# Cached keys turned once per page and stored, values copied by page ahead: paged attention with a LoRA layer behind it, on one core

## The chip, the cores and the metric

One core of a Trainium2 chip runs the kernel. The metric is the device time of one execution in microseconds.

## The reference, cut to what matters

Two layers on x (8 batches of 128 tokens, 512 wide), all in float32. The first is attention over a paged cache: 32 query heads, 8 key/value heads of 128, so one key/value head serves four query heads (REP). A batch has 16 cache pages of 32 keys, named by a block table, and 128 new keys.

```python
q = _rope(_rmsnorm(x @ Wq.T)); k = _rope(_rmsnorm(x @ Wk.T)); v = x @ Wv.T
kc = k_cache[block_table].reshape(bsz, 512, 8, 128)      # 16 pages of 32 keys
vc = v_cache[block_table].reshape(bsz, 512, 8, 128)
k_all = concatenate([kc, k], axis=1); v_all = concatenate([vc, v], axis=1)
scores = where(valid, einsum('bqhd,bkhd->bhqk', q, k_all) * SCALE, -1e30)
o = einsum('bhqk,bkhd->bqhd', softmax(scores), v_all)
x = x + o.reshape(bsz, 128, 4096) @ Wo.T
```

The second layer is a 512 x 512 product with a gated mixture of two of eight low-rank experts. It runs after the last attention step and is not touched.

## The kernel before, in words

The program is written out by hand: each engine has its own list of instructions, and semaphores order them. The work is a loop of G = 64 steps s, one for each pair of key/value head s // 8 and batch s % 8. One step has 640 keys (512 cached, 128 new) and 4 query heads. Products are made in three passes of float32r: every operand is split by ACT into a high part (a Copy that rounds) and by DVE into a low part (`low`, L857: full minus high), and PE multiplies high by high, high by low and low by high (L320).

PE's order in step s (`step`, L1423): scores of heads 0 and 1; the query projection of group s + 2; scores of head 2; the product O of step s - 1 with the values; scores of head 3; the turns (transposes) of the probabilities of heads 0, 1, 2 (T0, T1, T2; `turn_probs`, L1390); the output projection Y; the turns of the queries, cached keys and new keys of group s + 1 (`turn_queries` L1356, `turn_cached_keys` L1368, `turn_new_keys` L1339); the key/value projection of s + 2; the turns of head 3's probabilities (T3) and of the new keys' ones (TN).

PSUM has four banks for this beside the scores' four, and each has several users in a fixed cycle (`BANKS`, L72); `wait_bank` (L296) makes PE wait until the user before has been copied out, by the table `FREES` (L288). QT is free when DVE has made qt_lo, Q when ACT has copied the queries (a_q).

```python
BANKS = (("Q", "T0", "QT", "T3"), ("O", "Y", "TN"), ("T1", "KTC"), ("T2", "KV"))
```

ACT's order in step s (L731): new keys and values copied, squares, exp and norm of heads 0 and 1, queries of s + 2 (`queries`, L642), exp and norm of head 2, the copy of O (L761), values (L698), probs 0 to 2 (L687), exp and norm of head 3, the split of w, then the high parts of turned queries, cached keys, new keys (L664 to L674), and the probabilities of T3 and TN. DVE (L1007) follows with the low parts, the row maxima (L952), the reciprocals (L962) and the rope's sine product (L927). POOL (L520) makes the rope's cosine product, the norms' weights and v_lo.

Cached keys and values come as one array `kv` in DRAM, rows of 256 numbers (128 of the key, 128 of the value), by head, page and slot. `kv_raw` in SBUF holds two groups. Groups 0 to 11 (GATHERED) are gathered by POOL with indirect DMAs, four for a group (L492), two steps ahead. Groups from 12 on are loaded by SP (`cached_pages`, L415): 16 DMAs for a group, one for each page, 32 rows of 1 KB, the page number read from SBUF into a register. SP's iteration s (L449) also loads a piece of w and of wo, and the split x of group s + 4 (`fetch_x`, L385), each behind waits that say its buffer is free; SP's queue keeps this order.

## Time and profile before

| | us |
|---|---|
| median of 3 runs | 1154.88 (1154.5 to 1155.11) |
| the profiled execution | 1157.93 |
| its span | 1156.1 |
| PE busy | 1144.5 (99%) |
| ACT busy | 927.9 (80%) |
| DVE busy | 907.1 (78%) |
| POOL busy | 550.3 (48%) |

The page of the profile gives the busy time of each engine, in all and in 40 slices, then the DMA queues, the chain of work that ended last, and the costliest groups of instructions. PE is matmul, PEld the weight load of PE, which overlaps it; "line" is a line of the kernel. In a timeline a row begins with start and length in us; rows of one kind are merged (x12), and brackets give the idle time before a row and who ended it. On ACT and DVE the next instruction may start some 0.1 us before the one before it has ended, so the distance of two starts is what an instruction costs its engine.

### The profile page before, as it was taken

What the parts mean: (1) busy time and instruction counts of PE and PEld (TensorE: products, weight loads), DVE (VectorE), ACT (ScalarE), POOL (GpSimd) and SP (SyncE); (2) the same over time, 40 slices, a digit from 0 to 9 for tenths busy, and PEclk for the clock granted to TensorE, in tenths of its full rate; (3) what the DMA queues carried; (4) which work ended last, traced back from release to release, by engine and by line L of the source; (5) the groups of instructions that cost most, each with busy time, mean ns of one, the idle gap of its engine ahead of it and who ended that gap; (6) DMA issues with size and microseconds to landing.
All of it is one profiled execution on the core that took longest, in us unless ns stands there. A gap on an engine that the chain in (4) does not pass through costs nothing.

```text
span 1156.1 us, 23349 instructions
## 1 busy us (share of the span) xinstructions
PE 1144.5 (99%) x6960; PEld 1030.6 (89%) x6960; DVE 907.1 (78%) x1883; ACT 927.9 (80%) x1833; POOL 550.3 (48%) x573
## 2 busy tenths in 40 slices
PE   8999999999999999999999999999999999999998
PEld 7888988989999998998998999899899899899997
DVE  8977788777778778777777877877877777777756
ACT  6887888888888888888888888888888888887751
POOL 5766766454444445345445444444534544544400
PEclk9999999999999999999999999999999999999999
DMA  7514322122223223222222322222222222221001
GB/s 244 166 61 138 102 88 96 58 88 80 77 87 93 65 87 90 68 87 88 86 72 87 94 63 87 92 66 88 89 69 86 87 84 71 85 81 53 23 1 73
DMA packets 86733, 98.31 MB, mean 85 GB/s; under 512 B 18768, under 2 KB 65744, under 8 KB 86480
## 3 DMA queue, kind: packets, MB, share of 16 engines
q1 hardware_dynamic: 84016, 90.40, 25.6%
q0 software_dynamic: 2304, 6.29, 1.7%
q8 instruction: 57, 0.93, 0.3%
q14 instruction: 68, 0.56, 0.2%
q10 hardware_dynamic: 288, 0.13, 0.0%
HBM read 90.45 MB, written 6.29 MB: 84 GB/s over the span
## 4 chain that ended last, share of the span: by engine, by line
PE 91%; ACT 3%; DVE 2%; issue 2%; DMA 0%; SPq 0%; POOL 0%; ACTq 0%; DVEq 0%; POOLq 0%
PE ps_s L1386 19%; PE ps_w L327 18%; PE ps_w L328 18%; PE ps_w L329 18%; PE ps_w L1397 9%; PE ps_w L1365 2%; PE ps_w L1406 2%; PE ps_w L1372 2%; ACT ps L679 1%; PE ps_s L1306 1%; DVE m L934 1%; PE ps_s L1340 1%; ACT ps L685 0%; DMA m<-wqkv 0%; DVE o_lo L858 0%
## 5 line engine op out<-in xcount | busy, mean ns | idle before, releaser
L685 ACT ACTIVATE ps<-ps,recip 128x640 f32<-128x640 f32 x256 | 213.3, 834 | 61.9 <-DVE recip L965 61.6
L858 DVE TENSOR_TENSOR pt_lo<-ps_w,pt_hi 128x512 fp32r<-128x512 f32 x322 | 204.4, 684 | 56.3 <-ACT pt_hi L690 53.4
L679 ACT ACTIVATE ps<-ps,negmax 128x640 f32<-128x640 f32 x256 | 213.3, 833 | 25.1 <-DVE negmax L958 24.0
L958 DVE CUSTOM_DVE_ANT_0 ps<-ps_s,mask 128x640 f32<-128x640 f32 x256 | 209.7, 820 | 8.0 <-issue 2.7
L507 POOL TENSOR_SCALAR meansq<-sumsq 128x5 f32<-128x5 f32 x63 | 12.8, 203 | 394.8 <-DVE sumsq L925 392.7
L690 ACT ACTIVATE pt_hi<-ps_w 128x512 fp32r<-128x512 f32 x256 | 139.5, 600 | 73.1 <-PE ps_w L1397 70.2
L327 PE MATMUL ps_w<-w_hi,xt_hi 128*128 128x512 f32 (+1 forms) x496 | 172.1, 347 | 0.0
L328 PE MATMUL ps_w<-w_lo,xt_hi 128*128 128x512 f32 (+1 forms) x496 | 167.3, 337 | 0.0
L329 PE MATMUL ps_w<-w_hi,xt_lo 128*128 128x512 f32 (+1 forms) x496 | 167.3, 337 | 0.0
L1397 PE MATMUL ps_w<-cst,ps 128*128 128x128 f32 x1024 | 133.2, 273 | 0.3 <-DVE qt_lo L858 0.2
L515 POOL TENSOR_TENSOR rot<-u,cos 128x640 f32<-128x640 f32 x63 | 100.6, 1597 | 66.2 <-DVE u L980 66.2
L533 POOL TENSOR_TENSOR rot<-rot,m 128x320 f32<-128x320 f32 x126 | 107.8, 879 | 50.6 <-DVE m L934 50.4
L327 PE MATMUL ps_w<-pt_hi,v_hi 128*128 128x512 f32 x320 | 125.4, 392 | 0.0
L328 PE MATMUL ps_w<-pt_lo,v_hi 128*128 128x512 f32 x320 | 125.2, 391 | 0.0
L329 PE MATMUL ps_w<-pt_hi,v_lo 128*128 128x512 f32 x320 | 124.5, 389 | 0.0
L1386 PE MATMUL ps_s<-kt_hi,qt_hi 128*128 128x320 f32 x512 | 122.2, 320 | 1.6 <-DVE kt_lo L858 1.6
L1397 PEld LDWEIGHTS ps_w<-cst,ps 128*128 128x128 f32 x1024 | 117.1, 141 | 1.7 <-ACT ps L685 0.9
L1386 PE MATMUL ps_s<-kt_hi,qt_lo 128*128 128x320 f32 x512 | 117.2, 310 | 0.0
L1386 PE MATMUL ps_s<-kt_lo,qt_hi 128*128 128x320 f32 x512 | 116.9, 309 | 0.0
L327 PE MATMUL ps_w<-wo_hi,o_hi 128*128 128x512 f32 x256 | 105.3, 411 | 2.6 <-DVE o_lo L858 2.4
L934 DVE TENSOR_TENSOR m<-u,sin 128x640 f32<-128x640 f32 x64 | 103.9, 1623 | 0.0
L329 PEld LDWEIGHTS ps_w<-w_hi,xt_lo 128*128 128x128 f32 x496 | 93.3, 188 | 10.0
(186 smaller groups left out, 2640.4 us busy)
## 6 DMA issues: line engine op xcount, KB each, us to landing
kv_raw<-kv SPq DMA_DIRECT2D x832, 32.0 KB, 1.6
xt_hi<-xsplit SPq DMA_DIRECT2D x56, 256.0 KB
xt_lo<-xsplit SPq DMA_DIRECT2D x56, 256.0 KB
w_raw<-wqkv SPq DMA_DIRECT2D x56, 192.0 KB, 3.4
wo_raw<-wo SPq DMA_DIRECT2D x56, 128.0 KB, 3.3
y<-xT SPq DMA_DIRECT2D x8, 256.0 KB, 3.1
y<-x SPq DMA_DIRECT2D x8, 256.0 KB
out<-y SPq DMA_DIRECT2D x8, 256.0 KB, 2.2
```

What stands on the lines that cost most here:

```text
L327: nc.tensor.matmul(out_ap, a_hi, b_hi, start=start and k == 0, stop=False)
L328: nc.tensor.matmul(out_ap, a_hi, b_lo, start=False, stop=False)
L329: last = nc.tensor.matmul(out_ap, a_lo, b_hi, start=False, stop=stop and k == n - 1)
L533: nc.gpsimd.tensor_tensor(rot[:, :, a:a + HALF], rot[:, :, a:a + HALF], m2[:, :, c:c + HALF], ALU.add).then_inc(p_rot, 1)
L679: nc.scalar.activation(ps[:, h, :], ps[:, h, :], ACT.Exp, bias=negmax[:, s % 2, h:h + 1], scale=-1.0, accum_out=rowsum[:, s % 2, h:h + 1]) ...
L685: nc.scalar.activation(ps[:, h, :], ps[:, h, :], ACT.Copy, scale=recip[:, s % 2, h:h + 1]).then_inc(a_norm, 1)
L690: nc.scalar.activation(pt_hi[:, 0:CT, h, :], probs_bank(s, h).rearrange("p (t q) -> p t q", t=CT), ACT.Copy).then_inc(a_pt, 1)
L858: return nc.vector.tensor_tensor(out_ap, full, hi.bitcast(F32), ALU.subtract)
L934: nc.vector.tensor_tensor(m2[:], u[:], sin[:, g % B, :].unsqueeze(1).to_broadcast([P, NH, D]), ALU.mult).then_inc(d_m2, 1)
L958: nc.vector.tensor_tensor_reduce(out=halves(ps[:, h, :]), in0=ps_s[:, h % 2, :, 0:KH], in1=halves(mask[:, s % B, :]), scale=-SCALE, scalar ...
L1386: last = nc.tensor.matmul(ps_s[:, h % 2, half, 0:KH], a, c[:, half * KH:(half + 1) * KH], start=n == 0, stop=n == 2)
L1397: last = nc.tensor.transpose(probs_bank(s, h)[:, t * S:(t + 1) * S], ps[:, h, t * P:(t + 1) * P], ident)
```

## The change

From the third head on (TURNED = 2, groups KG = 16 and up) cached keys are no longer turned in the step that uses them. The cache holds 64 pages a head. In steps 5 to 52 PE turns, once for each head, eight natural pages (256 rows: two transposes, `turn_natural_keys`), ACT copies them to `k_turned`, and SP stores them by page in a DRAM array `kT` (128 x 32 numbers a page). From group 16 on SP loads a group's 16 turned pages from `kT` into the keys' half of `kv_raw` (`key_pages`; 128 rows of 128 B each), and ACT and DVE split them right from SBUF; PE's four transposes of the cached keys are not there in those steps. The values of heads 2 to 7 are copied in DRAM in steps 5 to 12, page by page in the order of the block table (`copy_values`: for each batch 16 DMAs, each 6 heads x 32 rows x 512 B), into `paged`; a group's values are then one load (`load_values`, 4 x 128 rows of 512 B). POOL gathers groups 0 to 15 in place of 0 to 11.

Order changes: the probabilities of heads 0 to 2 are turned and split in the order 1, 0, 2 (TURNS); ACT's copy of the queries stands behind the copy of O, not before exp of head 2; from group 16 on the cached keys' split stands on ACT and DVE between probs and exp of head 3 (DVE: reciprocal), and ACT's split of w behind the new keys and the natural copy. PE's natural turn stands behind the new keys' turn, in the bank of the scores of heads 1 and 3; the scores of head 1 of the next step wait for ACT's copy of it. The negated sines are not made; sine and its negative become one table, with a subtract for the first half of the rope.

```diff
-GATHERED = 12
+TURNED = 2
+KG = TURNED * B
+TPAGES = PAGES // B
+TT = TPAGES * PSIZE // P
+AHEAD = 3
+TURNS = (1, 0, 2)
+COPY = 5
...
+        k_nat = sb("k_nat", [P, TT, D])
+        k_turned = sb("k_turned", [P, TPAGES, PSIZE])
+        kT = nc.dram_tensor("kT", (HK * PAGES, D, PSIZE), F32).ap()
+        paged = nc.dram_tensor("paged_values", (B, HK - TURNED, NPP, PSIZE, D), F32).ap()
...
-        sin = sb("sin", [P, B, D])
+        sin = sb("sin", [P, B, HALF])
...
+        def naturals(s):
+
+            n = s + AHEAD
+            return n if KG - B <= n < (HK - 1) * B else None
+
+        def key_cols(g):
+            return kv_raw[:, g % 2, :, 0:D]
+
+        def tiles_of(keys):
+            return keys.rearrange("p (t q) -> p t q", t=CT)
+
+        def naturals_bank():
+            return ps_s[:, 1, 0, 0:TT * P]
...
+        def turn_number(s, h):
+
+            return TURNS.index(h) + 1 if s > 0 and h in TURNS else h + 1
...
-            def cached_pages(g):
-
-                wait(sp, pe_ktc, g - 2)
+            def natural_keys(s):
+                n = naturals(s)
+                if n is None:
+                    return
+                if n > KG - B:
+                    sp.wait_ge(pe_nat, n - (KG - B))
+                row = (n + B) * TPAGES * PSIZE
+                sp.dma_start(k_nat[:], kv[row:row + TT * P, 0:D].rearrange("(t p) d -> p t d", t=TT)).then_inc(s_knat, 16)
+
+            def keep_keys(s):
+                n = naturals(s)
+                if n is None:
+                    return
+                sp.wait_ge(a_nat, n - (KG - B) + 1)
+                page = (n + B) * TPAGES
+                sp.dma_start(kT[page:page + TPAGES].rearrange("n d s -> d n s"), k_turned[:]).then_inc(s_kstored[(n // B + 1) % 2], 16)
+
+            def page_numbers(b, part):
+                at = I_BLOCK + b * CT
+                _, ids = nc.values_load_multi_w_load_instructions(
+                    cin[part * PSIZE:part * PSIZE + 1, at:at + CT], engines=[mybir.EngineType.SP], min_val=0, max_val=PAGES - 1,
+                    skip_runtime_bounds_check_because="pages of the table are numbered from 0 to PAGES - 1")
+                return ids
+
+            def copy_values(b):
+
+                pages = kv.rearrange("(h n s) d -> n h s d", h=HK, s=PSIZE)
+                for part in range(PPT):
+                    ids = page_numbers(b, part)
+                    for t in range(CT):
+                        sp.dma_start(paged[b, :, t * PPT + part, :, :],
+                                     pages[bass.ds(ids[t], 1), TURNED:HK, :, D:2 * D].rearrange("o h s d -> (o h) s d")
+                                     ).then_inc(s_paged, 16)
+
+            def load_values(g):
+                if g == KG:
+                    sp.wait_ge(s_paged, 16 * B * NPP)
                 wait(sp, p_v, g - 2, 2)
-                pages = kv.rearrange("(n s) d -> n s d", s=PSIZE)
+                sp.dma_start(kv_raw[:, g % 2, :, D:2 * D],
+                             paged[g % B, g // B - TURNED].rearrange("n s d -> (n s) d").rearrange("(t p) d -> p t d", p=P)
+                             ).then_inc(s_values[g % 2], 16)
+
+            def key_pages(g):
+
+                wait_stored(sp, g // B, B)
+                wait(sp, d_ktc, g - 2)
                 for part in range(PPT):
-                    at = slice(part * PSIZE, (part + 1) * PSIZE)
-                    b = I_BLOCK + g % B * CT
-                    _, ids = nc.values_load_multi_w_load_instructions(
-                        cin[part * PSIZE:part * PSIZE + 1, b:b + CT], engines=[mybir.EngineType.SP], min_val=0, max_val=PAGES - 1,
-                        skip_runtime_bounds_check_because="pages of the table are numbered from 0 to PAGES - 1")
+                    ids = page_numbers(g % B, part)
                     for t in range(CT):
-                        sp.dma_start(kv_raw[at, g % 2, t, :], pages[bass.ds(ids[t] + g // B * PAGES, 1)].rearrange("o s d -> (o s) d")
-                                     ).then_inc(s_pages[g % 2], 16)
+                        sp.dma_start(kv_raw[:, g % 2, t, part * PSIZE:(part + 1) * PSIZE],
+                                     kT[bass.ds(ids[t] + g // B * PAGES, 1)].rearrange("o d s -> (o d) s")
+                                     ).then_inc(s_keys[g % 2], 16)
...
+                if s > 0:
+                    keep_keys(s - 1)
+                natural_keys(s)
...
-                if GATHERED <= s + 2 < G:
-                    cached_pages(s + 2)
+                if 0 <= s - COPY < B:
+                    copy_values(s - COPY)
+                if KG <= s + 2 < G:
+                    key_pages(s + 2)
+                    load_values(s + 2)
```

ACT's step afterwards (the other engines alike):

```diff
-                if has(g2):
-                    queries(g2)
                 if has(s) and s >= G - HB + 1:
                     final_turn(s - (G - HB + 1))
                 if has(s):
@@ -759,24 +851,33 @@
                     wait(act, pe_o, s - 1)
                     wait(act, pe_y, s - 2)
                     nc.scalar.activation(o_hi[:], bank("O"), ACT.Copy).then_inc(a_o, 1)
+                if has(g2):
+                    queries(g2)
                 if has(s):
 
                     values(s)
-                    probs(s, 0)
-                    probs(s, 1)
-                    probs(s, 2)
+                    for h in TURNS:
+                        probs(s, h)
                     if s in W_MID:
                         w_split(W_MID[s])
                     if s in WO_MID:
                         wo_split(WO_MID[s])
+                    if KG <= g1 < G:
+                        cached_keys(g1)
                     exps(s, 3)
                     norm(s, 3)
-                for n in W_AT.get(s, ()):
-                    w_split(n)
+                if g1 < KG:
+                    for n in W_AT.get(s, ()):
+                        w_split(n)
                 if has(g1):
                     turned_queries(g1)
-                    cached_keys(g1)
+                    if g1 < KG:
+                        cached_keys(g1)
                     new_keys(g1)
+                natural_keys(s)
+                if g1 >= KG:
+                    for n in W_AT.get(s, ()):
+                        w_split(n)
```

## Rows read from the trace of the kernel before

**Rows 1.** The page's part 1: busy us, share of the span, instructions, by engine
```profile
PE 1144.5 (99%) x6960; PEld 1030.6 (89%) x6960; DVE 907.1 (78%) x1883; ACT 927.9 (80%) x1833; POOL 550.3 (48%) x573
```

**Rows 2.** The stage table: us, busy us (instructions) by engine, clock, DMA share, GB/s
```profile
600.00:1000.00 400.00, 400.00 (x2446) 361.26 (x2445) 316.33 (x634) 332.69 (x658) 181.27 (x186) 1.00 0.27 81
```

**Rows 3.** Timeline of PE in step 34: start us, us, line, output and inputs
```profile
603.22 0.54 PE L1386 MATMUL ps_s<-kt_hi,qt_hi 128*128 128x320 f32 x2
...
611.88 0.39 PE L329 MATMUL ps_w<-pt_hi,v_lo 128*128 128x512 f32 x1
...
620.27 0.54 PE L1386 MATMUL ps_s<-kt_hi,qt_hi 128*128 128x320 f32 x2
```

**Rows 4.** The chain that ended last, PE's cached-key turns of step 34: start, us
```profile
617.66 0.44 PE ps_w L1372 x4
```

**Rows 5.** Timeline of ACT, at the start and in steps 33 and 34
```profile
29.12 1.54 ACT L685 ACTIVATE ps<-ps,recip 128x640 f32<-128x640 f32 x2
...
603.06 0.60 ACT L690 ACTIVATE pt_hi<-ps_w 128x512 fp32r<-128x512 f32 x1 [1.16 <-PE ps_w L1397]
...
609.60 0.58 ACT L645 ACTIVATE raw<-ps_w 128x512 f32<-128x512 f32 x1
610.07 0.83 ACT L679 ACTIVATE ps<-ps,negmax 128x640 f32<-128x640 f32 x1
...
612.31 0.60 ACT L761 ACTIVATE o_hi<-ps_w 128x512 fp32r<-128x512 f32 x1 [0.26 <-PE ps_w L329]
612.80 0.62 ACT L703 ACTIVATE v_hi<-kv_raw 128x512 fp32r<-128x512 f32 x1
613.33 0.30 ACT L704 ACTIVATE v_hi<-raw 128x128 fp32r<-128x128 f32 x1
613.62 1.58 ACT L690 ACTIVATE pt_hi<-ps_w 128x512 fp32r<-128x512 f32 x3
615.07 0.85 ACT L679 ACTIVATE ps<-ps,negmax 128x640 f32<-128x640 f32 x1
...
616.27 0.83 ACT L685 ACTIVATE ps<-ps,recip 128x640 f32<-128x640 f32 x1 [0.26 <-DVE recip L965]
617.01 0.51 ACT L582 ACTIVATE w_hi<-w_raw 128x384 fp32r<-128x384 f32 x1
```

**Rows 6.** Timeline of PE's weight loads, at the start and in step 34
```profile
29.99 0.42 PEld L1397 LDWEIGHTS ps_w<-cst,ps 128*128 128x128 f32 x4 [0.45 <-ACT ps L685]
...
612.84 1.38 PEld L1397 LDWEIGHTS ps_w<-cst,ps 128*128 128x128 f32 x12
...
619.38 0.46 PEld L1397 LDWEIGHTS ps_w<-cst,ps 128*128 128x128 f32 x4
```

**Rows 7.** Timeline of DVE in step 34
```profile
614.28 1.88 DVE L858 TENSOR_TENSOR pt_lo<-ps_w,pt_hi 128x512 fp32r<-128x512 f32 x3
...
618.32 0.69 DVE L858 TENSOR_TENSOR qt_lo<-ps_w,qt_hi 128x512 fp32r<-128x512 f32 x1 [0.38 <-ACT qt_hi L666]
```

**Rows 8.** Groups by line and shape, DVE's split of SBUF columns: busy us, mean ns
```profile
L858 DVE TENSOR_TENSOR w_lo<-w_raw,w_hi 128x512 fp32r<-128x512 f32 x2 | 1.4, 692 | 0.1
```

**Rows 9.** Timeline of SP: the page loads issued by iteration 33
```profile
599.98 9.43 SPq L427 DMA_DIRECT2D kv_raw<-kv  x16
```

**Rows 10.** SP's DMA issues by line: least/median/largest ns
```profile
L427 SPq DMA_DIRECT2D kv_raw<-kv x832: 315/316/1371, 207.8 to 1088.6; - x167
...
L375 SPq DMA_DIRECT2D y<-xT x8: 540/546/669, 0.7 to 45.1; - x8
```

**Rows 11.** DMA queues from 44 to 52 us, x loads of 512 B pieces: packets, MB, share
```profile
q1 hardware_dynamic: 1077, 0.53, 22.8%
```

**Rows 12.** DMA queues from 120 to 137 us: packets, MB, share of 16 engines
```profile
q1 hardware_dynamic: 576, 0.85, 16.2%
q0 software_dynamic: 192, 0.52, 8.4%
```

**Rows 13.** The page's part 3, the SP queue over the span: packets, MB, share
```profile
q1 hardware_dynamic: 84016, 90.40, 25.6%
```

More of the change, by code:

```diff
@@ L316, in wait_bank @@
                 if has(s + off):
+                    if freed is d_pt and nth <= REP:
+                        nth = turn_number(s + off, nth - 1)
                     wait(pe, freed, s + off, per, nth)
@@ L531, in step @@
                     wait(pool, d_m2, g1)
-                    for a, c in ((0, HALF), (HALF, 0)):
+                    for a, c, op in ((0, HALF, ALU.subtract), (HALF, 0, ALU.add)):
                         nc.gpsimd.tensor_tensor(rot[:, :, a:a + HALF], rot[:, :, a:a + HALF],
-                                                m2[:, :, c:c + HALF], ALU.add).then_inc(p_rot, 1)
+                                                m2[:, :, c:c + HALF], op).then_inc(p_rot, 1)
                 if has(s):
@@ L668, in cached_keys, with natural_keys @@
             def cached_keys(g):
-                wait(act, pe_ktc, g)
-                nc.scalar.activation(kt_hi[:, 0:L], bank("KTC"), ACT.Copy).then_inc(a_ktc, 1)
+                if g < KG:
+                    wait(act, pe_ktc, g)
+                    nc.scalar.activation(kt_hi[:, 0:L], bank("KTC"), ACT.Copy).then_inc(a_ktc, 1)
+                else:
+                    wait_keys(act, g)
+                    wait(act, pe_s, g - 1, 4)
+                    nc.scalar.activation(tiles_of(kt_hi[:, 0:L]), key_cols(g), ACT.Copy).then_inc(a_ktc, 1)
+            def natural_keys(s):
+                n = naturals(s)
+                if n is None:
+                    return
+                act.wait_ge(pe_nat, n - (KG - B) + 1)
+                if n > KG - B:
+                    wait_stored(act, (n - 1) // B + 1, (n - 1) % B + 1)
+                nc.scalar.activation(k_turned[:].rearrange("p n s -> p (n s)"), naturals_bank(), ACT.Copy).then_inc(a_nat, 1)
             def new_keys(g):
@@ L942, in cached_keys @@
                 wait(dve, a_ktc, g)
-                low(kt_lo[:, 0:L], bank("KTC"), kt_hi[:, 0:L]).then_inc(d_ktc, 1)
+                if g < KG:
+                    low(kt_lo[:, 0:L], bank("KTC"), kt_hi[:, 0:L]).then_inc(d_ktc, 1)
+                else:
+                    low(tiles_of(kt_lo[:, 0:L]), key_cols(g), tiles_of(kt_hi[:, 0:L])).then_inc(d_ktc, 1)
             def new_keys(g):
@@ L1061, in step @@
                     rowmax(s, 3)
-                    probs(s, 0)
-                    probs(s, 1)
-                    probs(s, 2)
+                    for h in TURNS:
+                        probs(s, h)
+                    if KG <= g1 < G:
+                        cached_keys(g1)
                     over_sum(s, 3)
@@ L1075, in step @@
                     turned_queries(g1)
[L1076 removed]
+                    if g1 < KG:
+                        cached_keys(g1)
                     new_keys(g1)
@@ L1206, in _ @@
             dve.wait_ge(d_cos, 1)
-            for a, c in ((0, HALF), (HALF, 0)):
-                nc.vector.tensor_tensor(rot[:, :, a:a + HALF], rot[:, :, a:a + HALF], m2[:, :, c:c + HALF], ALU.add).then_inc(d_rot, 1)
+            for a, c, op in ((0, HALF, ALU.subtract), (HALF, 0, ALU.add)):
+                nc.vector.tensor_tensor(rot[:, :, a:a + HALF], rot[:, :, a:a + HALF], m2[:, :, c:c + HALF], op).then_inc(d_rot, 1)
             dve.wait_ge(d_rot, 2)
@@ L1373, in turn_cached_keys, with turn_natural_keys @@
                 last.then_inc(pe_ktc, 1)
+            def turn_natural_keys(s):
+                n = naturals(s)
+                if n is None:
+                    return
+                pe.wait_ge(s_knat, 16 * (n - (KG - B) + 1))
+                wait(pe, d_max, s, 4)
+                for t in range(TT):
+                    last = nc.tensor.transpose(naturals_bank()[:, t * P:(t + 1) * P], k_nat[:, t, :], ident)
+                last.then_inc(pe_nat, 1)
             def scores(s, h):
+                if h == 1 and s > 0 and naturals(s - 1) is not None:
+                    pe.wait_ge(a_nat, naturals(s - 1) - (KG - B) + 1)
                 if h == 0:
@@ L1454, in step @@
                     scores(s, 3)
-                    turn_probs(s, 0)
-                    turn_probs(s, 1)
-                    turn_probs(s, 2)
+                    for h in TURNS:
+                        turn_probs(s, h)
                 if has(s - 1):
```

38 lines of the change are left out of this document (22 added, 16 removed).

## The prediction

> **What bounds the kernel now.** I read the page's busy shares first: PE is busy 99% of the span, DVE 78%, ACT 80%, POOL 48% [rows 1]. Then the stage table: from 600 to 1000 us PE is busy in every microsecond, at a granted clock of 1.00 [rows 2]. So time goes only with work taken off PE, or comes with a stall put into it. Last the timelines of one step, step 34 (a step is one head of one batch): it begins with its first scores at 603.22 and the next at 620.27, 17.05 us [rows 3]. PE runs its fixed order without a gap, so what counts of the other engines is how late they hand PE something; two of these margins the change touches.
>
> **Work taken from and given to PE.** Turning the cached keys of a step is four transposes, 0.44 us [rows 4]. They fall away from step 15 on, where group 16 would be turned: 48 x 0.44 = 21.1 us. The new natural turns are two transposes of the same shape, 0.22 us, in steps 5 to 52: 48 x 0.22 = 10.6. Net 10.6 us of PE work less: steps 5 to 14 get +0.22, steps 15 to 52 -0.22, steps 53 to 62 -0.44. That is the most the change can bring; whether it brings it hangs on two handovers.
>
> **First handover: queries and T0.** Q, T0, QT and T3 share one PSUM bank, so the turn of head 0's probabilities may start only when ACT has copied the queries out. Today that copy starts at 609.60 and has 3 us of margin. The change puts it behind the copy of O. That one starts at 612.31, as PE's last O product ends (611.88 + 0.39) [rows 3], and releases ACT 0.49 later; the queries' copy takes 0.58: done at 613.38 [rows 5]. A weight load that waits for ACT starts 0.05 after ACT's end: the first of two norms starts at 29.12 and takes 0.82 (its x2 row: 1.54 for both, 0.72 apart), to 29.94, and the load follows at 29.99 [rows 5, 6]. That makes 613.43. PE now turns head 1 first; its weight loads start at 612.84, twelve in 1.31 us, four in 0.44, so head 0 is wanted at 613.28 [rows 6]. It comes 0.15 late; nothing hides that.
>
> **Second handover: turned queries and T3.** T3 waits in the same bank until DVE has made qt_lo. Today qt_lo starts at 618.32, takes 0.69, and is seen at 619.06, 0.32 ahead of T3's first load at 619.38 [rows 6, 7]. The cached-key turn stood between the queries' turn and T3 and was this wait's cover: without it T3 is wanted at 619.38 - 0.22 = 619.16, from step 53 on at 618.94. And the ACT chain before it grows. From O's copy at 612.31, by the distances of the starts [rows 5]: O 0.49, queries 0.47 (609.60 to 610.07), values 0.53 and 0.29, three probs 1.45, cached keys now from SBUF like the values 0.53; exp starts at 616.07, norm 1.20 after it. DVE is later than that: the first pt_hi ends at 614.10 + 0.60, three pt_lo follow 0.60 apart from 614.73 and the cached kt_lo from 616.53 to 617.13 (512 columns from SBUF cost 0.69, as from PSUM [rows 7, 8]), then the reciprocal; norm at 617.33 in place of 617.27. Norm 0.74, qt_hi 0.60, 0.03, qt_lo 0.69, 0.05: T3 may load at 619.44. (The w split, 0.51 on ACT, has been moved behind this and is counted out.) That is 0.06 later than today: all of the 0.22 or 0.44 is waited away and a little more. T0's delay lies inside this chain, since PE waits later anyway. Bounds of a step from 15 on: -0.22 or -0.44, plus 0.15, if the chain has room; +0.2 if each of its dozen links costs 0.01 more. I take +0.06, as each link has its row.
>
> **The other edits.** ACT's natural copy stands behind qt_hi, where ACT waited 1.16 us for T3 [rows 5]: room for 256 columns (at most the 0.60 of 512) and the w split; scores of head 1, which now wait for it, come later still. The sign copy of the sines, one ACT instruction at the start, goes: 0 to -0.6 us (512 columns), taken 0, since it has other work beside it. Subtract costs what add did. Four more steps of gathers on POOL fall into its idle half [rows 1]. SP: 16 page loads take 9.43 us of it today [rows 9], 0.59 each, with 0.32 for the issue of 32 rows; the dearest short issue is the 512-piece load's 0.55 [rows 10]. So 16 loads of 128 rows cost 9.4 to 13.1 us; I take the middle, 11.3. Seven others (values, two of x, w, wo, natural, stored) at 0.55 at most: 3.9. Together 15.2 of 17.05. SP's new waits: the stored keys wait for ACT's natural copy of the step before, and behind them stand the natural load, w, wo, pages and x. The natural load goes out some 1.5 us into a step and PE wants it at 14.3. The pages wait for kt_lo of two groups back, done; they are out by 17 and ACT wants them 12 us into the next step. Key pages are 16 x 128 pieces of 128 B a step; a piece of 512 B costs a DMA engine 27 ns (1077 packets in 22.8% of 16 x 8 us [rows 11]), so over 16 engines these take 3.5 us at most, beside 25% of 17 = 4.2 today [rows 12]. The 128 value copies, DRAM to DRAM, stand in steps 5 to 12, each of 192 pieces of 512 B: over 16 engines 16 x 12 x 27 ns = 5.2 us a step. Both fit beside the rest.
>
> **The sum.** Steps 1 to 4: 4 x 0.15 = 0.6. Steps 5 to 14, where the old turn still covers T3: 10 x (0.22 + 0.15) = 3.7. Steps 15 to 61: 47 x 0.06 = 2.8. Step 62, with no queries to copy: -0.4. Total +6.7. The profiled execution took 1157.93 (span 1156.1 and 1.8 around it) and would take 1164.6. The median of the runs lies 3.05 below it, so I forecast 1154.88 + 6.7 = 1161.6.
>
> **Rivals.** (a) Faster: the chain to T3 has room. For it: ACT idles a fifth of the span; 0.3 us less in the chain frees PE. Against: no link of it overlaps in the rows. Then steps 15 to 52 give 38 x (0.15 - 0.22) = -2.7, steps 53 to 61 9 x (0.15 - 0.44) = -2.6, step 62 -0.4, the early steps still +4.3: 1153.5, no change. With T0 unhindered too it is the whole -10.6: 1144.3.
> (b) Slower: the value copies load six engines. A copy has six outer pieces (heads) of 32 rows. If it is dealt by heads, six engines carry 16 x 32 x 27 ns = 13.8 us a step, with today's 4.2 and 1.4 of natural and stored keys (16 + 64 pieces an engine, at the 27 ns or half of it) 19.4, against a step of 17.4: 2 us of backlog more a step. PE's natural turn, at 14.3, needs a load issued at 1.5 behind that backlog; less 2 us to land and 4 of the copies before, 7 us are free, used up by step 9; from then to step 13 PE stalls 2 us a step: +8, 1170. No row shows a piece from DRAM to DRAM. Not less than 27 ns is seen; at the queue's mean packet, 56 ns (25.6% of 16 x 1156.1 us over 84016 [rows 13]), a step needs 34 us: +16 for eight steps, 1290. I take 27. For it: the outer counts are 6 and 32, not 128. Against: nothing here shows a transfer on fewer than 16.
> The Trainium skill, "DMA: Bandwidth & Descriptors", section "Why a DMA increments its semaphore by 16 and not by 1", says that a transfer uses the largest number of engines up to 16 that divides the slowest dimension of both sides; for six that is six, and the time would be (b)'s. The transfers of this trace have 32 or 128 outer rows, so no run here shows it.
> (c) Slower: SP becomes the bound. At 0.05 us above 0.55 for a page load, SP needs 0.8 us more than a step: 47 x 0.8 = +38, 1200. Against: the 512-piece load is no dearer [rows 10].
>
> **How the numbers follow.** Forecast 0.43, own range 1154 to 1168 (47 steps, each +-0.1 to 0.15). Rival (a) 0.22, spread from 1144 to 1154; most of it ends with T0 partly free, below 1152.5. (b) at 27 ns or a little more, 1168 to 1190, 0.22. (b) with a dearer piece, or (c), above 1190: 0.13. A measurement of this kernel tells 0.2%, 2.3 us, from no change. Within it lie 0.09 of the forecast and 0.04 of (a). So faster 0.18, same 0.13, slower 0.69. The range leaves out 0.08 below 1147 and 0.12 above 1190.
>
> **What would show it.** Right: 96 fewer transposes on PE, and still 17.1 us a step from 15 on, with weight loads of the probabilities' turn waiting for DVE's qt_lo there and for ACT's queries copy in the early steps; SP and POOL as before. Wrong by (a): no such waits and steps of 16.85, then 16.6. Wrong by (b): PE waits in steps 8 to 13 for the natural keys, and steps of 19 us. Wrong by (c): SP without idle, and ACT waiting for key pages.

## The result, and the profile after

The changed kernel takes **1197.5 us** (median of 4 runs, 1194.8 to 1199.5), the kernel before took 1155.0 beside it (4 runs, 1154.5 to 1156.7): ratio **1.0366** [1.0353, 1.0379], 42.5 us slower. I had forecast 1161.6 and a range that ended at 1190. The sign was right, the size was not. Two runs far slower than all others of the same kernel are compared with none: the second of e2_thin (1272 us, at a granted clock of 0.85) and one of the kernel before beside e3 and e6 to e8 (2326 us).

The page of the changed kernel, part 1 (busy us, share of the span, instructions) and part 4 (what the chain that ended last consists of):

```profile
PE 1155.5 (96%) x6864; PEld 1028.7 (86%) x6864; DVE 931.5 (78%) x1883; ACT 936.9 (78%) x1880; POOL 567.6 (47%) x593
...
PE 81%; SPq 11%; DVE 3%; issue 2%; ACT 1%; DMA 1%; POOL 0%; ACTq 0%; DVEq 0%; POOLq 0%
```

PE has its 96 transposes fewer than in [rows 1], and yet is busy 11 us longer, at 96% instead of 99. New is SPq: 11% of the time that sets the end is SP putting DMAs into its queue. Where it lies, the stage table tells (us, then busy us and instructions of each engine, granted clock, DMA share, GB/s):

```profile
137.00:154.00 17.00, 16.84 (x105) 14.89 (x104) 13.67 (x28) 13.88 (x30) 11.34 (x12) 1.00 0.39 113
154.00:171.00 17.00, 7.87 (x48) 7.33 (x47) 4.30 (x10) 5.19 (x13) 4.62 (x7) 0.70 0.58 174
171.00:188.00 17.00, 13.69 (x76) 11.62 (x75) 13.35 (x27) 12.79 (x26) 11.69 (x13) 1.00 0.51 140
188.00:205.00 17.00, 16.88 (x92) 15.35 (x93) 12.31 (x30) 11.78 (x23) 7.30 (x8) 0.90 0.38 113
205.00:260.00 55.00, 43.20 (x241) 38.54 (x241) 30.65 (x60) 32.46 (x66) 29.06 (x33) 0.89 0.54 154
260.00:300.00 40.00, 34.09 (x200) 29.94 (x198) 27.78 (x54) 28.76 (x57) 24.00 (x26) 0.97 0.51 146
300.00:600.00 300.00, 299.61 (x1790) 267.66 (x1791) 240.88 (x469) 250.17 (x504) 134.95 (x139) 0.99 0.40 99
600.00:1000.00 400.00, 399.93 (x2394) 355.87 (x2394) 327.30 (x636) 338.11 (x682) 186.07 (x190) 1.00 0.39 95
```

From 300 us on it is the picture of [rows 2], PE without a gap. The loss lies between 154 and 300 us. I set the two kernels side by side step by step (distance between the starts of the new keys' probability turn, the last thing that PE turns in a step):

```
step            7      8      9     10     11     12     13     14   sum 7-14   15 to 60, each
before       17.45  17.05  17.57  17.06  17.06  17.05  17.06  17.05   137.35      17.05
after        28.20  21.85  23.84  20.22  25.77  19.74  23.67  17.96   181.25      17.00
```

Eight steps lose 43.9 us; the 46 steps from 15 to 60 together gain 2.3. In the first of the eight, PE stands for 9.1 us at the turn of the natural keys (timeline of PE, idle time and its releaser in brackets):

```profile
165.63 0.69 PE L1489 MATMUL ps_s<-cst,k_nat 128*128 128x128 f32 x2 [9.13 <-DMA k_nat<-kv]
```

From 110 to 310 us PE waits for nothing else (us in all, times, longest):

```profile
PE ps_s L1489 <- DMA k_nat<-kv: 30.8, 8, 9.1
```

The eight waits are 30.8 us of the loss. The rest goes with PE's longer busy time: around and behind the gaps the stage table has granted clocks of 0.70 to 0.97 in four of its stretches.

The DMA is named, but it isn't slow (3.6 us from issue to landing, by the page). It is issued late, as SP's own timeline shows (start us, us, line, what it issues):

```profile
140.87 0.33 SPq L454 DMA_DIRECT2D wo_raw<-wo  x1
141.92 16.95 SPq L486 DMA_DIRECT2D paged_values<-kv  x16
158.93 0.47 SPq L431 DMA_DIRECT2D xt_hi<-xsplit  x1
159.45 0.41 SPq L432 DMA_DIRECT2D xt_lo<-xsplit  x1
159.91 0.43 SPq L471 DMA_DIRECT2D kT<-k_turned  x1
160.38 0.96 SPq L463 DMA_DIRECT2D k_nat<-kv  x1
161.39 0.65 SPq L445 DMA_DIRECT2D w_raw<-wqkv  x1
162.08 0.90 SPq L454 DMA_DIRECT2D wo_raw<-wo  x2
163.71 17.52 SPq L486 DMA_DIRECT2D paged_values<-kv  x16
```

**This is the main reading of the case.** Sixteen value copies keep SP for 17 us, as long as PE's whole step, and SP has 5 us of other issues a round. The natural keys, which PE wants at 156, go out at 160.4, behind the copies of the round before. From the second round of copies (141.92) to the eighth (276.35) there are six rounds in 134.4 us: **22.4 us a round** against a step of 17.4. One copy is priced by the view of its line (ns least/median/largest), beside the page loads of 128 rows and the values' load:

```profile
L486 SPq DMA_DIRECT2D paged_values<-kv x128: 692/711/908, 114.8 to 292.8; - x128
...
L505 SPq DMA_DIRECT2D kv_raw<-kT x768: 332/333/1864, 308.3 to 1111.6; - x192
...
L494 SPq DMA_DIRECT2D kv_raw<-paged_values x48: 382/425/436, 318.3 to 1119.6; - x48
```

The balance: one long round from the first to the second row of copies (114.79 to 141.92, 27.1 us, 9.7 over a step) and six that are 5.0 over it make 39.8, against the 42 that steps 7 to 14 lose beyond their 17.4. The long round isn't all issue: 5.7 us of it are the load of the output weights (at 135.5), most of that a wait for its buffer.

### The profile page after: what moved, and what is told of

It is laid out like the page before. It is cut to its first block, busy times and chain, and to the rows that moved or that the text cites. A ratio compares the mean times of both kernels' runs of the same rounds, so it can differ in the third digit from the quotient of the medians.

```text
span 1197.6 us, 23720 instructions
## 1 busy us (share of the span) xinstructions
PE 1155.5 (96%) x6864; PEld 1028.7 (86%) x6864; DVE 931.5 (78%) x1883; ACT 936.9 (78%) x1880; POOL 567.6 (47%) x593
## 4 chain that ended last, share of the span: by engine, by line
PE 81%; SPq 11%; DVE 3%; issue 2%; ACT 1%; DMA 1%; POOL 0%; ACTq 0%; DVEq 0%; POOLq 0%
PE ps_s L1505 16%; PE ps_w L369 16%; PE ps_w L368 16%; PE ps_w L370 16%; PE ps_w L1516 9%; SPq L486 8%; PE ps_w L1525 2%; PE ps_w L1472 2%; SPq L475 2%; PE ps_s L1413 1%; PE ps_s L1489 1%; SPq L445 1%; PE ps_s L1447 0%; DMA k_nat<-kv 0%; SPq L471 0%
## 5 line engine op out<-in xcount | busy, mean ns | idle before, releaser
L368 PE MATMUL ps_w<-w_hi,xt_hi 128*128 128x512 f32 (+1 forms) x496 | 174.5, 352 | 0.0
L1516 PE MATMUL ps_w<-cst,ps 128*128 128x128 f32 x1024 | 145.3, 278 | 2.5 <-ACT raw L725 1.0
L1034 DVE TENSOR_TENSOR m<-u,sin 128x640 f32<-128x640 f32 x64 | 122.8, 1919 | 0.0
L370 PEld LDWEIGHTS ps_w<-w_hi,xt_lo 128*128 128x128 f32 x496 | 96.1, 194 | 10.1
```

Source lines behind the costliest of these rows:

```text
L368: nc.tensor.matmul(out_ap, a_hi, b_hi, start=start and k == 0, stop=False)
L370: last = nc.tensor.matmul(out_ap, a_lo, b_hi, start=False, stop=stop and k == n - 1)
L1034: nc.vector.tensor_tensor(m2[:].rearrange("p h (t d) -> p (h t) d", t=2), u[:].rearrange("p h (t d) -> p (h t) d", t=2), sin[:, g % B, :]. ...
L1516: last = nc.tensor.transpose(probs_bank(s, h)[:, t * S:(t + 1) * S], ps[:, h, t * P:(t + 1) * P], ident)
```

## The experiments

Theory 1: SP's issuing of the copies is the loss, and its price hangs on the outermost count (the number of pieces in the first loop of the transfer). Theory 2, the rival: the transfers load too few DMA engines (the prediction's rival (b)). Theory 3: an issue is dear because it has 192 pieces or goes from DRAM to DRAM. The times below are medians; each ratio is to the kernel before on the same chip.

| kernel | us | ratio |
|---|---|---|
| after | 1197.5 | 1.0366 [1.0353, 1.0379] |
| e1_spread | 1166.2 | 1.0096 [1.0079, 1.0113] |
| e2_thin | 1189.7 | one run |
| e4_no_copies | 1157.0 | 1.0019 [1.0010, 1.0029] |
| e6_spread_before_wo | 1158.6 | 1.0037 [1.0021, 1.0052] |
| e3_spread_queries_back | 1155.4 | 1.0005 [0.9995, 1.0015] |
| e7_before_queries_late | 1189.9 | 1.0301 [1.0280, 1.0321] |
| e12_heads_in_order | 1188.5 | 1.0289 [1.0270, 1.0307] |
| e8_spread_wo_queries | 1150.4 | 0.9963 [0.9949, 0.9977] |
| e9_eleven_steps | 1155.7 | 1.0007 [0.9998, 1.0016] |
| e10_eleven_steps_six | 1160.2 | 1.0043 [1.0028, 1.0059] |
| e13_nine_steps | 1161.5 | 1.0030 [1.0016, 1.0043] |
| e14_nine_steps_again | 1161.7 | 1.0032 [1.0019, 1.0045] |
| e15_wo_queries_again | 1163.4 | 1.0050 [1.0031, 1.0068] |
| e16_six_wo_queries | 1185.4 | 1.0233 [1.0219, 1.0248] |
| e17_no_copies_queries | 1153.1 | 0.9958 [0.9942, 0.9975] |
| e18_wo_queries_third | 1163.4 | 1.0060 [1.0038, 1.0083] |

### Rows outermost

```diff
-sp.dma_start(paged[b, :, t * PPT + part, :, :],
-             pages[bass.ds(ids[t], 1), TURNED:HK, :, D:2 * D].rearrange("o h s d -> (o h) s d")
+sp.dma_start(paged[b, :, t * PPT + part, :, :].rearrange("h s d -> s h d"),
+             pages[bass.ds(ids[t], 1), TURNED:HK, :, D:2 * D].rearrange("o h s d -> (o s) h d")
```

> The same copies with the 32 rows of a page as the outermost count of the transfer (32 x 6 pieces of 512 B, instead of 6 x 32). Theory 1 (SP's issuing of the value copies makes the stage slow, and its price hangs on the outermost count, 6): an issue falls from 0.71 us to the 0.33 to 0.45 us of the transfers of 128 rows, 16 of them with their register loads from 17.3 us to 10 to 13, SP's round in steps 5 to 12 from 22.5 us to 15.5 to 18.5, and the time from 1197.5 to 1153 to 1163 us. Theory 2 (six DMA engines are overloaded, the issue price is the same as before): the issues stay at 0.71 us, yet the time falls to about 1155 us. Theory 3 (an issue is dear because it copies from DRAM to DRAM, or has 192 pieces): issues stay at 0.71 us and the time at 1190 to 1200 us.

1166.2 us: with the same pieces and bytes, 31 of the 42.5 us are gone. The issue costs 553 ns at the median instead of 711, not the 0.35 to 0.45 that I expected, and the sixteen take 13.4 to 14.4 us; SP's round is 18.2 us ((250.99 - 141.80) / 6). A price set by the 192 pieces, one half of theory 3, is out, since these are 192 pieces too; so is one set by DRAM to DRAM alone. Theories 1 and 2 aren't told apart by this run alone: the form changes both the issue and, perhaps, the number of engines. Its steps 8 to 14 are at 17.4 to 18.3, but step 7 is still 26.1 us long.

### An eighth of the bytes, the form kept

```diff
-sp.dma_start(paged[b, :, t * PPT + part, :, :],
-             pages[bass.ds(ids[t], 1), TURNED:HK, :, D:2 * D]...
+sp.dma_start(paged[b, :, t * PPT + part, 0:4, :],
+             pages[bass.ds(ids[t], 1), TURNED:HK, 0:4, D:2 * D]...
```

> The outermost count stays 6, but only 4 of the 32 rows of each page are copied (24 pieces, an eighth of the bytes); the values of steps 16 to 63 are loaded from rows of the cache in their own order, so the gather of the values is left out. Theory 1: SP's issues stay at 0.65 to 0.71 us each, its round at 22 us, the time at 1190 to 1198 us. Theory 2 (six DMA engines overloaded): an eighth of the pieces lets the late key and weight transfers through, 1153 to 1160 us. Theory 3 (price of 192 pieces): the issue falls towards 0.4 us, SP's round to 17 to 18 us, 1153 to 1163 us; if it is the price of DRAM to DRAM it stays, and this run can't tell it from theory 1.

1189.7 us, from one run. The view of the copies' line in this kernel, and two rows of its SP timeline:

```profile
L486 SPq DMA_DIRECT2D paged_values<-kv x128: 693/710/908, 114.5 to 287.1; - x128
```

```profile
162.45 17.54 SPq L486 DMA_DIRECT2D paged_values<-kv  x16
184.23 17.15 SPq L486 DMA_DIRECT2D paged_values<-kv  x16
```

Seven eighths of the transfer are gone and the issue costs the same 710 ns, the round 21.6 us, and the time falls by 8 us of 42. PE still waits 25.2 us for the natural keys, 30.8 in the change. **That decides between the theories**, on one run but by a wide margin: the rival asked for 1153 to 1160. Only those 8 us are left for the transfers.

### No copies at all

```diff
-                if 0 <= s - COPY < B:
-                    copy_values(s - COPY)
```

> No value copies at all; the values of steps 16 to 63 are loaded from rows of the cache in their own order, so the gather of the values is left out. Every theory that puts the loss on the copies: steps 7 to 14 go back from a mean of 22.7 us to 17.1, and with the steady step of 17.00 us (17.05 before) the time is 1151 to 1155 us. If the turn of the key pages (PE, its eviction, k_nat's load) were itself late, steps 7 to 14 would keep over 17.5 us and the time would be 1158 us or more.

1157.0 us, a little above the range. Without copies most of steps 5 to 14 take 17.40 us, +0.35 on the 17.05 of before, as my working of the two handovers had it, and the later ones 17.01. Before's own profile has some of the early steps long (17.52, 17.45 and 17.57 in the fifth, seventh and ninth, 17.98 and 18.09 in the third and fourth), so over the ten steps the difference is +2.4, not +3.5; with -0.04 in 46 steps that is +0.6, and the medians are 2.0 apart. That profile was of an execution 3 us above its median, so the early steps of the two can't be compared to a microsecond. By the medians the copies cost 40.5 of the 42.5 us.

### The price of a form

One kernel in which each of the eight copy steps copies in another shape (outermost count x inner pieces of 512 B):

> Each of the eight copy steps copies a part of each page in another shape, outermost count x inner pieces of 512 B: 6x32, 32x6, 6x4, 16x6, 1x32, 8x6, 3x32, 12x6; the values of steps 16 to 63 are loaded in the cache's own order, so the gather of the values is left out. Theory 1 (price by the outermost count): 0.71, 0.35 to 0.45, 0.65 to 0.71, 0.35 to 0.45, over 0.8, 0.55 to 0.65, over 0.75, 0.5 us. Theory 3 (price by pieces): in the order of 192, 192, 24, 96, 32, 48, 96, 72 pieces, so that the third and the fifth are the cheapest; if it is the price of DRAM to DRAM, all are about 0.7 us.

The view of the issuing line, narrowed to one step at a time, in the order 6x32, 32x6, 6x4, 16x6, 1x32, 8x6, 3x32, 12x6:

```profile
L503 SPq DMA_DIRECT2D paged_values<-kv x16: 699/706/908, 115.1 to 132.2; - x16
...
L503 SPq DMA_DIRECT2D paged_values<-kv x16: 553/553/1072, 141.7 to 154.9; - x16
...
L503 SPq DMA_DIRECT2D paged_values<-kv x16: 698/716/817, 160.7 to 177.6; - x16
...
L503 SPq DMA_DIRECT2D paged_values<-kv x16: 553/553/628, 182.6 to 195.3; - x16
...
L503 SPq DMA_DIRECT2D paged_values<-kv x16: 492/492/538, 200.1 to 212.3; - x16
...
L503 SPq DMA_DIRECT2D paged_values<-kv x16: 656/663/773, 216.8 to 232.5; - x16
...
L503 SPq DMA_DIRECT2D paged_values<-kv x16: 697/708/811, 237.2 to 254.0; - x16
...
L503 SPq DMA_DIRECT2D paged_values<-kv x16: 767/770/881, 258.7 to 276.1; - x16
```

The number of pieces does nothing: 192 and 24 pieces with outermost count 6 are 706 and 716 ns, 192 and 96 with 32 and 16 both 553. Nor is it the copy from DRAM to DRAM, which all eight share. Counts 16 and 32 are cheap; 6, 3, 8 and 12 are dear, 663 to 770, and not in the order of the counts, as I had expected. The 1x32, which I put among the dearest, is the cheapest: a leading count of one evidently doesn't count. What fits all eight is whether the outermost count above one is 16 or 32. The register load between the copies follows it (median of a step's loads of page numbers, 6x32 and then 1x32):

```profile
L475 SPq TENSOR_LOAD <-cin x3: 801/807/982, 119.3 to 128.5; - x3
...
L475 SPq TENSOR_LOAD <-cin x3: 302/307/750, 202.8 to 209.8; - x3
```

So sixteen copies of 6x32 take 17.8 us of SP, of 1x32 12.7. The Trainium skill, "DMA: Bandwidth & Descriptors", section "Why a DMA increments its semaphore by 16 and not by 1", says that a transfer on k engines, k below 16, leaves it to the issuing sequencer to write the other 16 - k increments. With the engines counted as the prediction quotes it, that draws the line where these rows have it; but it would order the prices 3, 6, 8, 12, and the rows have 12 on top, so it isn't the price list. That these increments are what costs is not shown by any run.

### Where on SP the copies stand

```diff
                 if 0 <= s - COPY < B:
                     copy_values(s - COPY)
                 for n in WO_AT.get(s + 1, ()):
                     wo_load(n)
-                if 0 <= s - COPY < B:
-                    copy_values(s - COPY)
```

> e1_spread (rows outermost), and on SP the 16 value copies of a step stand ahead of the load of the last output-weight piece instead of behind it. Theory 1, its second half: what e1_spread still lost in step 7 (26.1 us for 17.4) is that SP first sat out that load's wait for its buffer (9 to 12 us, idle) and only then issued 13.6 us of copies; with the copies in that idle time steps 7 and 8 fall to 17.4 and 17.4 to 17.7 us, and the time from 1166.2 to 1156 to 1158 us, that of the kernel without copies. Rival: the transfers themselves (6144 B-pieces of 512 B a step next to the weight loads) make the keys late; then step 7 or another one keeps 3 us or more and the time stays above 1160 us.

Steps 7 and 8 fall to 17.43 and 17.42 us as expected, the time to 1158.6, a little above the range. So 7.6 of the remaining 9 us of e1_spread were idle time of SP spent at the wrong place: it waited there for DVE to free the output weights' buffer while the copies, which wait for nothing, stood behind. In step 7 of e1_spread (first row) that wait is in the 8.96, here (second row) the same load is issued at once after the copies:

```profile
132.11 8.96 SPq L454 DMA_DIRECT2D wo_raw<-wo  x2
141.80 13.40 SPq L486 DMA_DIRECT2D paged_values<-kv  x16
```

```profile
133.55 13.84 SPq L486 DMA_DIRECT2D paged_values<-kv  x16
147.44 0.59 SPq L454 DMA_DIRECT2D wo_raw<-wo  x1
```

Steps 11 and 12 still take 17.9 and 18.5 us: the round of 18.2 us outlasts the step of 17.4, and the lead is used up by then.

### The queries' copy

```diff
+                if has(g2):
+                    queries(g2)
                 if has(s) and s >= G - HB + 1:
                     final_turn(s - (G - HB + 1))
...
                     nc.scalar.activation(o_hi[:], bank("O"), ACT.Copy).then_inc(a_o, 1)
-                if has(g2):
-                    queries(g2)
```

> e1_spread, with ScalarE's copy of the queries back where it was, ahead of the exponential of head 2. Theory A (the first turn of probabilities waits for it, 0.16 us a step): the steady step falls from 17.00 to 16.85 us in all steps from 5 on, the time by 58 x 0.15 = 8.7 us to 1157 to 1158 us. Rival B (the last turn, which waits for qt_lo, takes over at once): the steady step falls by 0.05 us or less and the time stays at 1163 to 1166 us. Rival C (the exponential of head 2 and what hangs on it, 0.5 us later, make the first turn later still): the step is 17.1 us or more, 1170 us or more.

The steady step falls from 17.01 to 16.83 us (16.77 from step 53 on), the time to 1155.4, 1.6 us below my range. Theory A holds. In the changed kernel the wait is seen each step at the head-0 turn, and it is gone in e8_spread_wo_queries (second fence), which has the queries back too:

```profile
655.28 0.51 PEld L1516 LDWEIGHTS ps_w<-cst,ps 128*128 128x128 f32 x4
655.96 0.86 PEld L1516 LDWEIGHTS ps_w<-cst,ps 128*128 128x128 f32 x8 [0.16 <-issue]
```

```profile
643.81 1.38 PEld L1516 LDWEIGHTS ps_w<-cst,ps 128*128 128x128 f32 x12
```

Then the same edit on the kernel before, and the new order of heads taken back:

> The kernel before with one edit of the change alone: ScalarE's copy of the queries stands behind o_hi instead of ahead of the exponential of head 2. Theory A: each step's first turn comes 0.15 us late, 17.20 us a step instead of 17.05, 60 x 0.15 = 9 us, 1163 to 1165 us. Rival: it is absorbed, 1154.5 to 1156 us.

> e1_spread with the probabilities turned in the order of heads 0, 1, 2 again (the change turns 1, 0, 2). Head 0's turn goes into the bank that the queries' copy frees. Theory: the change's order hides 4 turns (0.44 us) of that wait; without it the first turn is 0.6 us late instead of 0.16, as in e7_before_queries_late (0.62), the steady step 17.45 us, the time 1166.2 + 58 x 0.44 = 1192 us. Rival: the order does nothing, 1164 to 1168 us.

e7 is a miss: 1189.9 us where I had 1163 to 1165. Every step takes 17.63 us, +0.58, since the kernel before turns head 0 first and meets the whole wait (timeline of PE's weight loads of this kernel):

```profile
646.88 1.29 PEld L1397 LDWEIGHTS ps_w<-cst,ps 128*128 128x128 f32 x12 [0.63 <-issue]
```

I had carried the 0.15 over from a kernel that turns head 1 first. e12 is the counterpart: 1188.5 us, steady step 17.41 instead of 17.01. The change's order 1, 0, 2 hides 0.4 us a step of a wait that its own move of the queries makes; leaving the queries where they were costs nothing.

### All three, and the copies spread over more steps

> e6 and e3 together: rows outermost, the copies ahead of the last output-weight load, the queries back in their place. Theory 1 with theory A: steps 7 to 14 at 17.25 us, the steady step at 16.85 us, 1147 to 1150 us, faster than the kernel before. With rival B: 1154 to 1157 us.

1150.4 us, ratio 0.9963: faster than both kernels, on that chip. Steps 7 and 8 take 17.26 us, the steady step 16.83. Steps 11 to 13 are left at 17.8, 18.0 and 18.2.

```diff
-                if 0 <= s - COPY < B:
-                    copy_values(s - COPY)
+                for u in range(max(0, 3 * (s - 3)), min(B * PPT, 3 * (s - 2))):
+                    copy_values(u // PPT, u % PPT)
```

> e8_spread_wo_queries, with the 128 value copies over steps 3 to 13, twelve a step, instead of sixteen a step over steps 5 to 12. Theory 1 (SP's round against PE's step): e8's round of 18.1 us (13.5 of copies and 4.6 of the rest) is still above PE's 17.26; with twelve copies it is 10.2 + 4.6 = 14.8 us and never late, so that steps 11 to 13 fall from 17.8, 18.0 and 18.2 to 17.26 us and the time from 1150.4 to 1147.5 to 1149 us. Rival (the copies' transfers are what is late there): the same bytes, so the same 2 us are lost elsewhere, 1150 us; or the earlier steps, in which more is loaded, lose 1 to 3 us, 1151 to 1153 us.

> e9_eleven_steps, but the copies in the change's own form, six heads outermost. Theory 1: twelve issues with their register loads take 13.2 us, the round 17.8 us against PE's 17.26; the lag grows by 0.5 us a step, 3 to 6 us in eleven steps, most of it taken up by the slack of the first steps: 1148 to 1153 us, against the 44 us that the same transfers cost in the change's own schedule. Rival (the six DMA engines' overload costs by itself, whoever issues): as many late pieces as in the change, 1165 us or more.

e9: steps 6 to 8 and 10 to 14 are all at 17.26 us, as a round of 14.8 us should give. But step 5 takes 25.0: the copies of steps 3 and 4 hold up the weights and the first natural keys (PE waits 5.95 us for them at 125.78), since in those steps SP has its own work and waits. Here my expectation missed (1155.7 us, not 1147.5 to 1149), and the rival named in it was right with more than it said. e10 missed too, 1160.2 us for 1148 to 1153. With the change's form it has the same 17.26 from step 7 on, and loses 13.4 us in its step 5 alone (30.6): twelve issues of the dear form, 12.5 to 13.0 us, plus the rest fit into a step. The twelve copies in these eleven steps fit the six-engine reckoning as well (three quarters of 13.8 us and 5.6 make 16), so e10 speaks for theory 1 only together with e2_thin.

### The same kernels on other chips

For nine steps (5 to 13, sixteen and twelve copies by turns) the edit is

```diff
+                for u in range(B * PPT):
+                    if s == COPY + u * 9 // (B * PPT):
+                        copy_values(u // PPT, u % PPT)
```

> e8_spread_wo_queries, with the copies over steps 5 to 13, sixteen and twelve a step by turns (14.2 on average). Theory 1: SP's round is 14.2 x 0.85 + 4.6 = 16.7 us on average, below PE's 17.26, and no step before the fifth is touched (e9_eleven_steps lost 7.7 us in its step 5 through the copies of its step 3). Every step from 6 to 14 at 17.26 us but the ninth (17.57 in every kernel, before too), so 2.2 us less than e8's 1150.4: 1147.5 to 1149 us. Rival: the 2 us turn up elsewhere, 1150 to 1151 us.

1161.5 us, against 1158.2 of the kernel before on that chip, where I had 1147.5 to 1149. Steps 3 to 14 are the long ones: 17.96 and 18.04 before the first copy, 17.7 in step 5, then 18.0 to 19.3, and 23.2 in step 7. So I repeated it beside e8's kernel and beside that with the change's form:

> The kernel of e13_nine_steps once more, beside e15 on one chip. Theory 1 (SP's round against PE's step is the whole loss): steps 11 to 13 at 17.26 us instead of 17.8, 18.0, 18.2, the time 2 us below e15's, 1147.5 to 1149 us on a chip on which the kernel before takes 1155. Rival: that the steps of 18.0 us from step 3 on come with the copies' place; then they are seen here again while e15 has 17.26 us, and the time is 1158 us or more.

> The kernel of e8_spread_wo_queries once more, as what e14 and e16 are held against: 1149.4 to 1151.5 us on a chip on which the kernel before takes 1155, its ratio to it 0.995 to 0.998.

> e15 with the change's own copy form, six heads outermost. Theory 1: SP's round is 17.3 + 4.6 = 21.9 to 22.3 us in eight steps against PE's 17.26, 8 x 4.8 = 38 us less the lead of one round with which SP starts (5 to 10 us): 1150.4 + 28 to 34 = 1178 to 1185 us. Rival (the order on SP and the queries' place were what mattered): under 1160 us.

This chip is of the same kind (before: 1157.2). e14 and e15, 1161.7 and 1163.4, differ by less than their runs scatter (1157 to 1164, 1159 to 1168), and neither beats the kernel before here. e16, 1185.4 us, puts the form alone at 22 us on equal footing, and its steps 6 to 12 take 21.0 to 23.4 us. SP's round there is 22.3 us, as theory 1 has it. But the wait that the profile shows isn't the one of the changed kernel's own profile. PE waits for the low parts of the probabilities, not once for the natural keys (110 to 310 us):

```profile
PE ps_w L368 <- DVE pt_lo L958: 24.1, 8, 3.6
```

The high part before it is late: ACT starts it 3.8 us after PE's turn has ended by PE's own row, and the profile can't name what released it ("remote"). Eight steps in a row have such a wait:

```profile
144.98 0.60 PE L1516 MATMUL ps_w<-cst,ps 128*128 128x128 f32 x4
149.35 0.60 ACT L784 ACTIVATE pt_hi<-ps_w 128x512 fp32r<-128x512 f32 x1 [4.83 <-remote]
```

e15 has the same in steps of 20 to 22 us (4.57 us at 147.03), the kernels on the first chip never. Whether the rows are misplaced there or the release itself was late, the profile doesn't tell. So e16 prices the form; by which wait it costs that on this chip is not shown. Last the kernel without copies, with the queries back, and e8's for the third time:

> e4_no_copies with the queries' copy back in its place: no value copies, the values of steps 16 to 63 loaded from rows of the cache in their own order, so the gather of the values is left out. If the copies are what makes steps 3 to 14 long on some chips: every step from 6 to 14 at 17.26 us (the ninth 17.57) whatever the chip, 1147.5 to 1149 us. If those steps are long for another reason: 18.0 us again on a chip on which the kernel before takes 1157 us, 6 to 9 us more in all, 1154 to 1158 us.

> The kernel of e8_spread_wo_queries for the third time, beside e17. On a chip on which the kernel before takes 1155 us: 1149.4 to 1151.5 us, ratio 0.995 to 0.998. On one on which it takes 1157 us or more: 1160 to 1165 us, ratio 1.002 to 1.007.

e17 shows the long steps without any copy: 17.97 and 17.94 in steps 3 and 4, 17.9 to 18.05 in steps 8 to 12. In step 3 PE waits for DVE's o_lo (weight loads of e17; the kernel before has the same wait in its own profile, 0.68 at 82.90, and its steps 3 and 4 take 17.98 and 18.09):

```profile
82.78 0.19 PEld L368 LDWEIGHTS ps_w<-wo_hi,o_hi 128*128 128x128 f32 x1 [0.69 <-DVE o_lo L954]
```

So the copies don't cause the 18 us. The o_lo is late because DVE is: in that step it starts its first row maximum 0.67 us late, and nothing that the profile shows released it:

```profile
73.79 0.82 DVE L1059 CUSTOM_DVE_ANT_0 ps<-ps_s,mask 128x640 f32<-128x640 f32 x1 [0.67 <-issue]
```

The same gap of 0.59 to 0.78 us stands in steps 3 to 5 of every profile with the long steps (e13 to e18, and before's own), in none of the others. What it is, no run shows. Beside it the copies cost more than on the first chip: e18 less e17 is 10.3 us here, while e8 lost 2.2 us to them (the excess of its steps 11 to 13 over 17.26). Why a chip has these steps at about 17.2 or at 18.0 stays open, and so does why the copies cost more there; it is a matter of 8 us, not of the 42.5.

## Why the prediction was wrong, point by point

**The failed step.** In "The other edits" I summed SP's issues for the steady stage (sixteen page loads and seven others, 15.2 of 17.05 us), and for steps 5 to 12 I costed the value copies on the DMA engines alone: 5.2 us a step, "both fit beside the rest". What sixteen copies cost SP was never summed. By the bounds that the same paragraph had for a page load, 0.59 to 0.82 us each, it would have been 9.4 to 13.1 us of a round; added to the others it wouldn't have passed 17.4, so the sum alone wouldn't have found the size. The dear form was what no row of before shows: 1.06 to 1.10 us a copy with its share of the register loads, 17 to 17.6 us for sixteen. The copies cost 40.5 of the 42.5 us (e4_no_copies), of which the form is 22 to 31 (e16 to e15, e1 to after) and the place behind the wait for the output weights 8 (e6 to e1).

**The sign** came right for another reason than the forecast's. Of the 6.7 us that the two handovers were to cost, the kernel without copies has 2.0, and its later steps are shorter than before's and not longer. "Slower" was right by luck.

**Rival (b)** described what was seen, waits of PE for the natural keys in steps 7 to 14, and even named the outermost count of six as the cause. Its mechanism was another: not a backlog on six engines but the issue. An eighth of the bytes took away 8 of 42.5 us (e2_thin, one run). How many engines a copy ran on, no view here shows. **Rival (c)**, SP as the bound, had the right engine and the wrong steps: the page loads of 128 rows cost 9.4 to 11.3 us for sixteen, 10.0 at the median, where I had taken 11.3, and from step 15 on SP never binds.

**PE's work.** 96 transposes fewer: right. That PE is busy longer all the same (1155.5 us against 1144.5 [rows 1]) goes with its waits: in the stretch from 154 to 171 us, 9.1 us of it idle, the granted clock is a mean of 0.70 of the 2.4 GHz level, where a stretch without a gap has 1.00. Without copies PE is busy 1142.9 us.

**First handover**, predicted 0.15 us late a step, nothing hiding it: measured 0.16, and 0.17 a step came back when the queries were moved back. Right, with the size. For steps 5 to 14 I had +0.37; without copies it is +0.35 in the steps that both profiles have even. Steps 2 to 4 take 17.22 to 17.31 us in the changed kernel and 17.06 to 17.20 with the queries back (e8).

**Second handover**, predicted +0.06 a step from 15 on, because qt_lo would come later than T3 is wanted: measured -0.05. The chain came 0.1 earlier than I had put it. From O's copy to qt_lo's start I had 6.39 us (links: norm at 5.02, then 0.74, 0.60, 0.03); in the changed kernel qt_lo starts at 644.02, and O's copy at 654.75 less a step of 17.00, 637.75, which is 6.27 before. The tenth is there at the first of the three low parts, 2.33 us after O's copy (640.08) where I had 2.42. So up to step 52 T3 doesn't wait visibly, and 17.00 is 17.05 - 0.22 + 0.16. From step 53, where another 0.22 falls away, it does wait, 0.24 us, and the step stays at 17.01:

```profile
1001.96 0.42 PEld L1516 LDWEIGHTS ps_w<-cst,ps 128*128 128x128 f32 x4 [0.24 <-issue]
```

The mechanism was right and only a tenth of a microsecond off; over 46 steps it is 5 us. Even with the queries back the later steps stay at 16.77, not 16.61: in e8 qt_lo ends at 1003.25 and T3's loads start at 1003.37, 0.33 behind the load before them, where the loads before came 0.12 apart. So this chain is the next bound there.

**The steady gain** that the change can bring was put at 10.6 us of PE work. With the three repairs it is seen as 0.22 a step (17.05 to 16.83), 4.5 us net on the one chip, and eaten up by the early steps on three others.

## What to carry to other kernels

When a change adds DMAs, sum what they cost the engine that issues them, round by round against the step of the bounding engine, and not only what they cost the DMA engines; a form of transfer that the trace doesn't show gets its own price there. Here a loop order in the transfer (32 outermost instead of 6) was worth 31 us and the place of the issues, ahead of a wait instead of behind it, another 8. An issue that waits for nothing doesn't belong behind one that waits.

## What the runs showed of the hardware

- The issue of a DMA on SP costs 492 or 553 ns where the outermost count above one was 16 or 32, and 656 to 770 where it was 3, 6, 8 or 12, whether it moved 24 pieces or 192. The page loads from DRAM to SBUF with 128 partitions cost 333.
- A register load on SP right behind copies of the dear forms takes 0.80 us, behind the 1x32 form 0.31.
- In some steps the time hangs on the chip. With the same instructions (e8, e15, e18) steps 3 and 4 took 17.1 and 17.2 us on one chip and 17.9 on two others, steps 6 to 10 took 17.3 to 17.6 us there and 18.0 to 21.8 here; without copies (e17) steps 8 to 12 still took 17.9 to 18.05. From step 15 on they agree to 0.02 us.
- The profiles of those chips have copies of ACT that start long after PE's row for their input has ended (3.8 us in e16), with a releaser that isn't named, and gaps of 0.6 to 0.8 us before a row maximum of DVE with none at all. What they are stays open.
